# Routing stage of a mixture-of-experts block: four row buffers, an unrolled norm, bias zeroing on ScalarE

## The reference

```
xn  = (x - mean) / sqrt(var + 1e-5)                      # per row of 256
out = x + time_mix(xn) + moe(xn)
moe: logits = xn @ gate_w.T + gate_b                     # 8 experts
     top 2 of softmax(logits) -> gates
     expert e: silu(xn @ w1e.T + b1e) * (xn @ w3e.T + b3e) @ w2e.T + b2e
     + a shared expert with hidden size 512
time_mix: k, v, r from xn, a recurrence over 2048 steps, an output projection
```

## Time and profile before

| | |
|---|---|
| median of 3 runs | 557.25 us (554.65 to 558.19) |
| the profiled execution | 556.1 us, its span 554.0 us |
| DVE, first `measure` of the norm half | starts at 10.62 us |
| DVE, first instruction of the choice half (line 634) | starts at 48.67 us |
| DVE, last wait of `route` over (line 737) | at 101.67 us |
| busy over the whole span | PE 85%, DVE 79%, POOL 48%, ACT 42% |

### The profile page before, as it was taken

How to read it: one execution, slowest core, us unless ns; L and a number is a source line. 1 busy time by engine, 2 the same in 40 slices (tenths; PEclk the granted TensorE clock), 3 DMA queues, 4 the chain that set the end, 5 groups by cost and what they waited for, 6 DMA issues and landing times. The chain is left out here.

```text
span 554.0 us, 10837 instructions
## 1 busy us (share of the span) xinstructions
PE 471.2 (85%) x2624; PEld 381.1 (69%) x2625; DVE 435.1 (79%) x963; ACT 234.7 (42%) x535; POOL 266.9 (48%) x312
## 2 busy tenths in 40 slices
PE   0668027499999999999999995989999999999997
PEld 0333013188878777777878784777889888988887
DVE  7877869357888888877888873899979696887974
ACT  0335334136656565555655563342232323242321
POOL 6000000353666666666565654878683754657300
PEclk9999555589999999999999998999999999999999
DMA  2798344138434333333333333924471817163111
GB/s 78 258 316 310 122 142 147 28 107 267 124 106 125 111 120 116 114 110 117 104 114 114 104 96 115 321 77 131 125 204 45 236 46 211 58 188 96 58 38 39
DMA packets 58553, 73.95 MB, mean 133 GB/s; under 512 B 6848, under 2 KB 47552, under 8 KB 58528
## 3 DMA queue, kind: packets, MB, share of 16 engines
q1 hardware_dynamic: 52048, 55.94, 30.8%
q0 software_dynamic: 6480, 17.70, 12.0%
HBM read 45.39 MB, written 28.18 MB: 133 GB/s over the span
## 5 line engine op out<-in xcount | busy, mean ns | idle before, releaser
L858 POOL DMA_INDIRECT xg<-xn_rows,picked x71 | 71.1, 1002 | 57.6 <-POOL picked L855 33.3
L1343 POOL DMA_INDIRECT yg<-expert_rows,rows x64 | 72.2, 1128 | 23.6 <-issue 17.1
L855 POOL COPY picked<-tile_tok 128x1 int32 (+1 forms) x71 | 13.9, 196 | 97.8 <-POOLq L315 93.2
L922 PE MATMUL ps_g<-w_hi,x_hi 128*128 x142 | 57.2, 403 | 0.9 <-DVE x_lo L1077 0.9
L922 PE MATMUL ps_g<-w_lo,x_hi 128*128 x142 | 56.6, 398 | 0.0
L922 PE MATMUL ps_g<-w_hi,x_lo 128*128 x142 | 56.5, 398 | 0.0
L1374 PE MATMUL ps_w<-col_hi,s_hi 128*128 128x512 f32 x128 | 51.1, 399 | 1.3 <-DVE res L1569 0.9
L1151 DVE RECIPROCAL rden<-den 128x128 f32<-128x128 f32 x32 | 30.3, 948 | 26.5 <-POOL den L872 26.5
L1375 PE MATMUL ps_w<-col_lo,s_hi 128*128 128x512 f32 x128 | 50.2, 392 | 0.0
L1376 PE MATMUL ps_w<-col_hi,s_lo 128*128 128x512 f32 x128 | 50.2, 392 | 0.0
L995 ACT ACTIVATE act<-ps_g 128x256 f32<-128x256 f32 x71 | 27.2, 383 | 52.0 <-PE ps_g L925 48.5
(11 more groups left out here) (199 smaller groups left out, 1421.8 us busy)
## 6 DMA issues: line engine op xcount, KB each, us to landing
expert_rows<-y SPq DMA_DIRECT2D x71, 128.0 KB
table<-mix_tables SPq DMA_DIRECT2D x16, 384.0 KB
raw_s<-x SPq DMA_DIRECT2D x16, 256.0 KB, 3.7
col<-xn_columns SPq DMA_DIRECT2D x8, 512.0 KB, 7.4
mix_tables<-coef SPq DMA_DIRECT2D x16, 256.0 KB
res<-x SPq DMA_DIRECT2D x16, 256.0 KB
out<-res SPq DMA_DIRECT2D x16, 256.0 KB
xn_rows<-raw_s SPq DMA_DIRECT2D x8, 256.0 KB, 3.7
```

The lines of the kernel that those rows point to most:

```text
L858: pool.indirect_dma_start(out=xg[a.buf(NG)][:], out_offset=None, in_=xn_d[:, :], in_offset=bass.IndirectOffsetOnAxis(ap=picked[a.buf(NG)][ ...
L922: nc.tensor.matmul(out, x[:, k, :], w[:, ds(e, 1), k, cols].rearrange("p o n -> p (o n)"), start=(k == 0 and n == 0), stop=False)
L1343: pool.indirect_dma_start(out=yg[a.buf(2)][:, k, q, :], out_offset=None, in_=y_d[:, :], in_offset=bass.IndirectOffsetOnAxis(ap=picked[a.bu ...
```

## The change

- x gets four buffers in place of two (`NX`): the first four loads are issued at the start, and `load_x(i)` waits for `norm(i-4)`.
- The loops of the norm half are unrolled. On DVE the order is now measure(i+1), norm(i), take(i-2). The order on PE stays turn(i), gate(i-1), back(i-2).
- The raw weights get eight buffers in place of four; four of them are the x buffers, and their loads are issued in the last four norm steps.
- The zeros of `bias_hl` are written by ACT, a block of 128 x 768 in each norm step, and no longer by GpSimd.
- On ACT, splits 0 and 1 stand ahead of the second exponential, 2 to 7 behind it, and one split stands behind each one-hot product. On DVE split 3 moves ahead of the batches.
- The stage's buffers have memory of their own; buffers of later stages are allocated behind it.

The core of the diff:

```diff
-        xin = [spare_x[:, b, :].rearrange("p (q c) -> p q c", q=Q) for b in range(2)]
-        xn = [spare_n0, spare_n1[:].rearrange("p k n -> p (k n)").rearrange("p (q c) -> p q c", q=Q)]
-        xT = [spare_t, sb("xT1", [P, KC, STEP], F32)]
-
-        NW = 4
-        w_raw = [t[:].rearrange("p k n -> p (k n)")[:, 0:WALL] for t in (spare_n0, spare_n1, *xT)]
-        later = spare_x[:].rearrange("p k n -> p (k n)")
-        maps = [later[:, n * NT * E:(n + 1) * NT * E] for n in range(7)]
+        NX = 4
+        xin = [sb(f"xin{b}", [P, Q, C], F32) for b in range(NX)]
+        xn = [sb(f"xn{b}", [P, Q, C], F32) for b in range(2)]
+        xT = [sb(f"xT{b}", [P, KC, STEP], F32) for b in range(2)]
+
+        NW = NX + 4
+        w_raw = [t[:].rearrange("p k n -> p (k n)")[:, 0:WALL] for t in (*xin, *xn, *xT)]
+        maps = [sb(f"map{n}", [P, NT * E], F32) for n in range(7)]
...
@@ -318,64 +317,60 @@
             def _(sp):
                 def load_x(a):
 
-                    at_least(sp, s_xn, a.i - 1)
+                    at_least(sp, s_xn, a.i - NX + 1)
                     for b in range(B):
-                        sp.dma_start(xin[a.buf(2)][:, b * HALF:(b + 1) * HALF, :],
+                        sp.dma_start(xin[a.buf(NX)][:, b * HALF:(b + 1) * HALF, :],
...
                                      xv[ds(a.i, 1), :, b, :, :].rearrange("o p h c -> p (o h) c")
-                                     ).then_inc(s_xin[a.buf(2)], 16)
-
-                def load_w(a):
-
-                    at_least(sp, s_wlo, a.i - NW + 1)
-                    sp.dma_start(w_raw[a.buf(NW)], wv[ds(a.i, 1)].rearrange("o p n -> p (o n)")
-                                 ).then_inc(s_w[a.buf(NW)], 16)
-
-                load_x(At(0, 0, 2))
+                                     ).then_inc(s_xin[a.buf(NX)], 16)
+
+                def load_w(i):
+
+                    at_least(sp, s_wlo, i - NW + 1)
+                    sp.dma_start(w_raw[i % NW], wv[ds(i, 1)].rearrange("o p n -> p (o n)")).then_inc(s_w[i % NW], 16)
+
+                load_x(At(0, 0, NSTEP))
                 sp.dma_start(gw[:], gate_w).then_inc(s_small, 16)
                 sp.dma_start(gb[:], gate_b.rearrange("(n a) -> n a", a=1)).then_inc(s_small, 16)
                 sp.dma_start(vec_tf[:], first).then_inc(s_small, 16)
                 sp.dma_start(vec_td[:], decay).then_inc(s_small, 16)
                 sp.dma_start(b_raw[:], b_all.rearrange("(p r) -> p r", p=P)).then_inc(s_small, 16)
-                load_x(At(0, 1, 2))
-
-                def step(a, more=True):
-                    at_least(sp, s_xn, a.i + 1)
-                    if more:
-                        load_x(a.plus(2))
+                for i in range(1, NX):
+                    load_x(At(0, i, NSTEP))
+
+                def step(a):
+                    sp.wait_ge(s_xn, a.i + 1)
+                    if a.i + NX < NSTEP:
+                        load_x(a.plus(NX))
                     for b in range(B):
                         sp.dma_start(xnv[ds(a.i, 1), :, b, :, :].rearrange("o p h c -> p (o h) c"),
                                      xn[a.buf(2)][:, b * HALF:(b + 1) * HALF, :]
                                      ).then_inc(s_xout[a.buf(2)], 16)
-                    at_least(sp, s_xT, a.i + 1)
+                    sp.wait_ge(s_xT, a.i + 1)
                     sp.dma_start(xT_d[:, ds(a.i, 1), :].rearrange("p o n -> p (o n)"),
                                  xT[a.buf(2)][:].rearrange("p k n -> p (k n)")
                                  ).then_inc(s_Tout[a.buf(2)], 16)
-
-                step(At(0, 0, 2))
-                step(At(0, 1, 2))
-                with sp.Fori(1, NSTEP // 2 - 1) as u:
-                    step(At(u, 0, 2))
-                    step(At(u, 1, 2))
-                step(At(NSTEP // 2 - 1, 0, 2), False)
-                step(At(NSTEP // 2 - 1, 1, 2), False)
+                    if a.i + NX >= NSTEP:
+                        load_w(a.i + NX - NSTEP)
+
+                for i in range(NSTEP):
+                    step(At(0, i, NSTEP))
...
-                    load_w(At(0, b, NW))
+                    load_w(NX + b)
...
-                    load_w(At(0, 2 + b, NW))
-                with sp.Fori(1, E * KC // NW) as u:
-                    for r in range(NW):
-                        load_w(At(u, r, NW))
+                    load_w(NX + 2 + b)
+                for i in range(NW, E * KC):
+                    load_w(i)
...
-                sp.wait_ge(s_bzero, 1)
+                sp.wait_ge(s_bzero, NSTEP)
...
-                nc.gpsimd.memset(bias_hl[:].rearrange("h e n -> h (e n)").bitcast(F32), 0.0).then_inc(s_bzero, 1)
                 nc.gpsimd.memset(pick2[:], 0.0).then_inc(s_two, 1)
...
-
-                def split(a):
-                    act.wait_ge(s_w[a.buf(NW)], (a.uses(NW) + 1) * 16)
-                    nc.scalar.activation(w_parts[0][:, ds(a.i, 1), :].rearrange("p o n -> p (o n)"),
-                                         w_raw[a.buf(NW)], ACT.Copy).then_inc(s_whi, 1)
+                    nc.scalar.activation(bias_hl[:, a.i, :].bitcast(F32), ident[:, 0:1].broadcast_to([P, WALL]),
+                                         ACT.Copy, scale=0.0).then_inc(s_bzero, 1)
+
+                def split(i):
+                    act.wait_ge(s_w[i % NW], (i // NW + 1) * 16)
+                    nc.scalar.activation(w_parts[0][:, i, :], w_raw[i % NW], ACT.Copy).then_inc(s_whi, 1)
 
                 act.wait_ge(s_small, 80)
                 act.wait_ge(s_const, 8)
-                root(At(0, 0, 2))
-                step(At(0, 0, 2), first=True)
-                step(At(0, 1, 2))
-                with act.Fori(1, NSTEP // 2 - 1) as u:
-                    step(At(u, 0, 2))
-                    step(At(u, 1, 2))
+                assert E == NSTEP
+                root(At(0, 0, NSTEP))
+                step(At(0, 0, NSTEP), first=True)
+                for i in range(1, NSTEP - 2):
+                    step(At(0, i, NSTEP))
+
...
                 def exps(n, first_step, last_step):
                     t = slice(first_step * Q, last_step * Q)
                     act.wait_ge(s_shift, n + 1)
                     nc.scalar.activation(score[:, t], work[:, t], ACT.Exp).then_inc(s_exp, 1)
 
-                step(At(NSTEP // 2 - 1, 0, 2))
+                step(At(0, NSTEP - 2, NSTEP))
                 exps(0, 0, EARLY)
-                step(At(NSTEP // 2 - 1, 1, 2), False)
-                logit(At(NSTEP // 2 - 1, 1, 2))
+                step(At(0, NSTEP - 1, NSTEP), False)
+                logit(At(0, NSTEP - 1, NSTEP))
+                split(0)
+                split(1)
                 exps(1, EARLY, NSTEP)
-                half = E * KC // 2
-                for n in range(half):
-                    split(At(0, n, half))
+                for i in range(2, NW):
+                    split(i)
                 for n in range(PAIRS // BATCH):
-                    if n < half:
-                        split(At(1, n, half))
-
                     act.wait_ge(s_hott, n + 1)
                     if n >= 2:
                         act.wait_ge(s_hotmm, n - 1)
                     nc.scalar.activation(hot_tok[n % 2][:, 0], hot_tile[n % 2][:], ACT.Copy, scale=row[:]
                                          ).then_inc(s_hotk, 1)
-                assert half == PAIRS // BATCH
+                    split(NW + n)
+                assert NW + PAIRS // BATCH == E * KC
...
-                turn(At(0, 0, 2))
-                turn(At(0, 1, 2))
-                gate(At(0, 0, 2))
-                turn(At(1, 0, 2))
-                gate(At(0, 1, 2))
-                back(At(0, 0, 2))
-                turn(At(1, 1, 2))
-                gate(At(1, 0, 2))
-                back(At(0, 1, 2))
-                with pe.Fori(2, NSTEP // 2) as u:
-                    turn(At(u, 0, 2))
-                    gate(At(u - 1, 1, 2))
-                    back(At(u - 1, 0, 2))
-                    turn(At(u, 1, 2))
-                    gate(At(u, 0, 2))
-                    back(At(u - 1, 1, 2))
-                gate(At(NSTEP // 2 - 1, 1, 2))
-                back(At(NSTEP // 2 - 1, 0, 2))
-                back(At(NSTEP // 2 - 1, 1, 2))
+                for i in range(NSTEP + 2):
+                    if i < NSTEP:
+                        turn(At(0, i, NSTEP))
+                    if 0 < i <= NSTEP:
+                        gate(At(0, i - 1, NSTEP))
+                    if i > 1:
+                        back(At(0, i - 2, NSTEP))
...
-                    dve.wait_ge(s_xin[a.buf(2)], (a.uses(2) + 1) * 32)
...
+                    dve.wait_ge(s_xin[a.buf(NX)], (a.uses(NX) + 1) * 32)
...
-                measure(At(0, 0, 2))
-                norm(At(0, 0, 2))
-                measure(At(0, 1, 2))
-                norm(At(0, 1, 2))
-                measure(At(1, 0, 2))
-                norm(At(1, 0, 2))
-                measure(At(1, 1, 2))
-                norm(At(1, 1, 2))
-                take(At(0, 0, 2))
```

(67 more changed lines are left out.)

12 lines of the change are left out of this document (6 added, 6 removed).

## The result

The changed kernel takes 569.85 us (median of 4 runs, 568.35 to 571.77) against 556.44 us for the kernel before on the same chip (4 runs, the three of the table above among them): a ratio of 1.024 (95% interval 1.019 to 1.029), so it is slower by 13.4 us. Its profiled span is 566.6 us, 12.6 more than before.

What follows compares the result with a forecast made beforehand. The prediction took DVE's chain through norms, choices and one-hot batches to bound the first 102 us. It added 20.0 - 6 = +14.0 us to the profiled 556.1, and 1.15 for the median: 571 us, range 562 to 581.

Steps and rivals of the forecast that it cites:

- Start: Start of the norm half: without GpSimd's zeros DVE's first cast ends 5.2 us earlier, first measurement at 5.4 us.
- The new wait: Norm half: behind each of norm(2) to norm(7) DVE waits 5.1 us for PE's burst, the first 1.7 us longer.
- The clock: TensorE in the norm half: each burst runs its first 3.4 us at half clock, the rest at full.
- half-clock rival: Norm half: every TensorE burst wholly at half clock, waits of 6.6 us, 580 us in all; chance 0.20.
- Choices: End of the norm half: DVE's choices start at 68.7 us against 48.67, 20.0 us later.
- Choice half: From the choices to the result: four terms, -1.0, -4.5, -1.3 and +0.9, sum -5.9 us, rounded to -6.
- Sum: Whole kernel: 20.0 us lost in the norm half less 6 won in the choice half, +14.0 us.
- The fast rival: Norm half: copies do not wait, DMAs need some 41 us; -14 us in all, 543 us; chance 0.05.

Runs made afterwards that it cites:

- zeros_pool: take_later with the zeros of `bias_hl` back on GpSimd in one memset, not on ScalarE; 546.8 us.
- pe_filled: The changed kernel with 26 more transposes of the identity as filling behind each TensorE burst from step 2 to step 6; 561.0 us.
- take_later: The changed kernel with DVE's copy of logits behind norm(i) being that of step i-3, as in the kernel before, not of step i-2; 544.03 us.
- choice_old: take_later with the choice half of the kernel before: four raw weight buffers, loads issued behind the norm half, old order of splits; 548.67 us.
- back_first: The changed kernel with back(i-2) ahead of turn(i) on PE, not behind gate(i-1); DVE's order kept; 544.14 us.

## Why the prediction was right

- **Start.** 5.4 us forecast, 5.90 measured. The price of the zeros was right: the cast became 5.16 us shorter, 5.2 forecast. What failed was the sentence that counted the small transfers as in by then: DVE waited for `b_raw`, and that took back 0.44 us. zeros_pool shows the cause of the 5.2.
- **The new wait** is the step on which the sign hung, and three runs show it from three sides: taking it away in DVE's order or in PE's gives 544 us, adding it alone to the kernel before gives 586. Six waits of 5.1 us and 1.7 for the first made 32.3; the trace has 33.3. This sum came out closer than its parts, and that is luck. The first wait was 5.15 us and not 6.8: turn(2) did start late, at 20.58 against the end of norm(2) at 18.96, but its burst then ran at full clock. The fourth and fifth were 6.30 and 6.41 and not 5.1. The errors, -1.65 and +2.5 us, nearly cancel; the other three, 4.97, 5.26 and 5.22, are as forecast.
- **The clock.** I took one dip of 3.4 us at half clock in every burst. The trace bears that out for three of the five bursts from 27.90 on (PEclk 0.70, 0.67 and 0.67). The other two (0.54 and 0.53) were at half clock for nearly all their length, and their waits are near the 6.6 us of the half-clock rival. pe_filled separates the two parts of the loss against take_later: 9 us is the clock, the other 17 (561.0 against 544.0) is that the engines alternate. The Trainium skill, "TensorE: Matmul & The Clock Gate", section "HAM oscillation — how this bites in real kernels", lets every burst after such a wait start cold. The trace agrees for three bursts (turns of 1.97 us at 27.90, 45.59 and 55.62) and not for a fourth: PE was idle for 3.82 us before 36.60 and the turn there still took 1.09 us, the fall came in the gate behind it.
- **Choices** at 69.00 us, forecast 68.7: +20.3 against +20.0. The end of norm(2) came 0.3 us later than forecast and the waits were 1.0 us longer, but DVE's own work between them was 16.7 us and not 17.7.
- **Choice half.** -5.9 forecast, 53.00 to 46.65 us measured, -6.35. By its parts: from the choices to the first batch 22.58 us became 22.19, -0.4 (-0.1 forecast, from -1.0 and +0.9); from there to the end of DVE's last piece 26.69 became 22.04, -4.65 (-4.5); from that piece to the result 3.73 became 2.42, -1.3 (-1.3). What is left of the waits in the batches are the two for splits 14 and 15, of which only the first is on the path. choice_old confirms the size with the norm half nearly unchanged: 5.4 us.
- **Sum.** `route` ends 14.0 us later, as forecast. The span grew by 12.6, because the rest of the program took 1.4 us less. Behind `route` the code is the same, and the same stretch took 454.05 us in take_later; which part of such differences is chance one profile each doesn't tell, and it stays open.
- **The fast rival.** I gave 543 us for a kernel in which the copies don't wait; take_later measures 544.03, and back_first, which is closer to the rival's words (back(i-2) is done when norm(i) ends), 544.14. take_later's norm half is held partly by DMA stores, as that rival said: choices at 40.72 us, where DVE alone would have been there at 36.4 by the sum of the prediction and the DMAs at 41.

## What to carry to other kernels

When an order is unrolled or shifted by one, check each wait against the order of the engine that it waits for: a result of step i-2 is two steps old only if the other engine has it in front of the work that you have just released. If it stands behind, the pipeline becomes a relay, and the idle engine may lose its clock on top. Extra buffers and a look-ahead belong together, and what they give is seen only when no wait of this kind is left: here the same edits were worth -13 us or +13 us by one place in an order.

## What the runs showed of the hardware

- A cast of 128x128 int32 on DVE took 6.29 us with GpSimd's memset of 5.22 us beside it (kernel before, zeros_pool) and 1.13 us where the memsets beside it took 0.99 us (two together) and 0.21. Its end, 8.86 us, lies right behind the long memset's, 8.64. That fits a wait for that instruction better than a slower rate; no run tells the two apart.
- After an idle time of 3.8 us TensorE's pieces ran at once at half clock (three bursts, turn 1.97 us) or began at full (one burst, 1.09 us) and fell within the gate; which of the two differed from round to round in one execution. After 1.79 us of idle time a burst (63.72) also began at full and fell within the gate. With 26 transposes as filling, and 1.0 us of idle time left, the granted clock was 1.00 in every burst behind a filling.
